# Margin check of a gated attention and expert kernel: its VectorE, ScalarE, TensorE and GpSimd pieces stand at other steps

## The chip, the cores and the metric

The kernel runs on one core of a Trainium2 chip. The metric is the device time of one execution in microseconds (us). Three runs of the kernel before gave 93.25, 93.72 and 95.69 us, median 93.72 us. One more execution, taken with the profiler, lasted 93.16 us; its span, from the first to the last instruction, is 91.4 us.

## The reference

Input x has 4 batches of 256 rows of 256 columns. It passes a gated layer pair and then a gated mixture of experts:

```
x = x + tanh(g_xattn) * GAT(ctx, adj = layernorm(x))      # two graph attention layers, 8 heads of 32
    e = leaky_relu(self + neigh) + -1e10 * (1 - adj);  alpha = softmax(e)
x = x + tanh(g_ffn) * MoE(layernorm(x))                   # 8 experts, hidden 128 each, top 2 of 8
    logits = tanh(xn @ Wg1.T) @ Wg2.T;  scores = softmax of the top 2, 0 elsewhere
    out = sum_e scores[e] * (silu(xn @ Wup[e].T + bup[e]) @ Wdown[e].T + bdown[e])
```

Since the mask factor is 1e10 and adj is a normalised row of x, the softmax picks in each row the column of the row's maximum, provided the maximum leads the second largest value by enough. The kernel uses that: it gathers rows by a one-hot matrix. The margin check proves that the lead of every row is large enough for the given weights. If it isn't, a general path recomputes everything.

## The kernel before

**Stages.** Up to about 30 us the kernel loads, finds each row's two largest values (`top`), builds the one-hot matrices and runs the two layers. Then `pe_experts`, `act_experts` and `dve_experts` run in step with each other, each as a loop over steps i written out by hand; the order of the calls in each is the order of that engine's queue. There are 32 work items (4 batches b of 8 experts e), and item k has its up product at step k (`pe_up`, L734 to L739), its SiLU on ScalarE at step k (L518), its weight broadcast (`pe_pick`, L756) at step k + 8, the product with it on VectorE (`dve_weigh`, writes `hid`, L1085) at step k + 8, the rounding copy on ScalarE (`act_hid`, L526) at step k + 8, the remainder (`dve_weigh_lo`, writes `hid_lo`, L1093) at step k + 9, and its down product (`pe_down`, L779 to L783) at step k + 11. Steps 32 and later have no up product.

**Once per batch.** The transposes of the next batch stand at e = 4 (`pe_xt`, L679), their rounding on ScalarE at e = 4 and the remainder `xt_lo` on VectorE (`dve_xt`, L1005) at e = 5. The router: gate product at e = 0 (`pe_gate`, L692), `dve_gate_sum` at e = 1, `dve_logits` at e = 2 (writes `lidx`), `scores` on GpSimd (L347 to L365), then two transposes on TensorE (`pe_score`, L700) and the copy `score_t` on VectorE (`dve_scores`, L1075) at e = 6. The first pick of the next batch, eight steps after the batch's first up product, waits for that copy. `dve_finish` (L1106) stands at e = 4 for the batch two behind.

**The margin check.** Its parts before the change:
- VectorE, step 13 (`check_peaks`, L1227 to L1233): maxima and sums of absolute values of ctx, W0, W1, the attention vectors and b0, six reductions, put into `peaks`. They stand ahead of `dve_xt` of step 13 and `score_t` of step 14.
- TensorE: transpose of `peaks` at the end of step 18 (`pe_peaks_turn`, L707), spread by a product with ones at the end of step 20 (`pe_peaks_spread`, L711). VectorE: `check_peak_max` at step 19 (L1238, L1241), `check_peaks_all` at step 21 (L1245).
- TensorE waits for `peaks_all` ahead of the score transposes of batch 2, step 22, since both use one PSUM bank.
- ScalarE: eight squares with row sums at steps 12 to 19 (L549).
- GpSimd: scores(2), `check_bound` (ten small operations), scores(3), `check_rows` (twelve small operations, each waiting for the one before). The first of `check_rows` waits for all eight squares.
- TensorE at step 37 (`pe_good_count`, L717) counts good rows, VectorE at step 38 makes the flag (L1250 to L1254), on which all engines branch.

Of the kernel before, what the change touches and what calls it, by code (L numbers as in the profile page):

```python
# [26 lines left out]
ALU = mybir.AluOpType  # L27
ACT = mybir.ActivationFunctionType
AX = mybir.AxisListType
# [7 lines left out]
B, N, D = 4, 256, 256  # L37
FIN = 64
H, FO = 8, 32
E, HE = 8, 128  # L40
T = B * N
NT = T // P
C = N // P
STEPS = B * E
# [3 lines left out]
SILU_SLOTS = PICK_LAG + 2  # L48
HID_SLOTS = 4
SCORE_PLACE = (3, 6, 6, 6)  # L50
WQ = 4
EQ = E // WQ
KS = 32 + 2 * E
# [9 lines left out]
def build(nc, x, ctx_t, w0, small, w1, bias_2, b0_r, b1_r, wup, wdown, bdown_2, check_w, avec, out):  # L63
    with ExitStack() as stack:
# [8 lines left out]
        ctx_sb = sb("ctx_sb", [P, T])  # L73
# [39 lines left out]
        peaks = sb("peaks", [P, P])  # L113
# [219 lines left out]
        def scores(pool, run, b):  # L333

            nb = run * B + b
            r = pair(b)
            done = [(run * (B - 1) + b - 1) * SCORE_STEPS]
            last = done[0] + SCORE_STEPS

            def link(ins, chained=True):  # L340
                done[0] += 1
                ins.then_inc(score_step, 1)
                if chained:
                    pool.wait_ge(score_step, done[0])

            pool.wait_ge(lidx_rdy, C * (nb + 1))
            link(nc.gpsimd.tensor_copy(lidx_f[:, r, 0:2], lidx[:, r, 0:2]))  # L347

            pool.wait_ge(lth_rdy, nb + 1)
            link(nc.gpsimd.tensor_scalar(prob[:, 0, r], lth[:, r], 0.5, 0.5, ALU.mult, ALU.add), False)  # L350
            link(nc.gpsimd.tensor_scalar(prob[:, 1, r], lth[:, r], -0.5, 0.5, ALU.mult, ALU.add))
            for k in range(2):
                for t in range(C * b, C * b + C):
                    link(nc.gpsimd.tensor_scalar(hit[:, k, t, :], expert_no[:], lidx_f[:, t, k:k + 1], prob[:, k, t:t + 1],
                                                 ALU.is_equal, ALU.mult), k == 1 and t == C * b + C - 1)
            link(nc.gpsimd.tensor_tensor(score[:, r, :], hit[:, 0, r, :], hit[:, 1, r, :], ALU.add))
            link(nc.gpsimd.tensor_copy(score_hi[:, r, :], score[:, r, :]))
            if run >= 1:
                pool.wait_ge(score_mm, run * B)
            if nb == 1:  # L360
                pool.wait_ge(score_zero, 1)
            hi, whole = (v.rearrange("p t (a e) -> p t a e", a=1).broadcast_to([P, C, 2, E])
                         for v in (score_hi[:, r, :].bitcast(F32), score[:, r, :]))
            nc.gpsimd.tensor_copy(score_parts[:, r, 0:2, 0:E], hi).then_inc(score_rdy, 1)
            nc.gpsimd.tensor_tensor(score_parts[:, r, 0:2, E:2 * E], whole, hi,  # L365
                                    ALU.subtract).then_inc(score_rdy, 1)
            assert done[0] == last

        @block.gpsimd
        def _(pool):  # L370
# [76 lines left out]
            def ts(o, a, *rest):  # L447
                link(nc.gpsimd.tensor_scalar(o, a, *rest))
# [17 lines left out]
            def check_rows():  # L466
                pool.wait_ge(xsq_rdy, NT)
                ts(rms[:], xsq[:], 1.0 / D, EPS, ALU.mult, ALU.add)
                tt(rms[:], rms[:], powers[:, NT:2 * NT], ALU.pow)
                tt(lead[:], top[:, :, 0], top[:, :, 1], ALU.subtract)  # L470
                ts(size[:], top[:, :, 0], -1.0, 0.0, ALU.mult, ALU.max)
                ts(good[:], top[:, :, 0], 0.0, None, ALU.max)
                tt(size[:], size[:], good[:], ALU.add)
                tt(size[:], size[:], rms[:], ALU.add)
                ts(size[:], size[:], 2e-6, None, ALU.mult)
                ts(need[:], rms[:], bound[:, 6:7], None, ALU.mult)
                tt(need[:], need[:], size[:], ALU.add)
                tt(lead[:], lead[:], need[:], ALU.subtract)
                nc.gpsimd.tensor_scalar(good[:], lead[:], 0.0, None, ALU.is_gt).then_inc(good_rdy, 1)

            scores(pool, 0, 2)
            check_bound()
            scores(pool, 0, 3)
            check_rows()

            def general():
                for b in range(B):
# [40 lines left out]
        def act_experts(act, run, extra):  # L528

            for i in range(STEPS + PICK_LAG):  # L530
                b, e = i // E, i % E
                if i < STEPS:
                    act_silu(act, run, i)
                    if b >= 1 and e == 2:
                        act_gate(act, run, b)
                    if b >= 1 and e == 3:
                        act_diff(act, run, b)
                if i >= PICK_LAG:
                    act_hid(act, run, i - PICK_LAG)
                if e == 2 and b + 1 < B:  # L540
                    act_norm(act, run, b + 1, range(C))
                if e == 4 and b + 1 < B:
                    act_xt(act, run, b + 1)
                for step in extra.get(i, ()):
                    step()
                if run == 0 and 12 <= i < 12 + NT:

                    t = i - 12
                    nc.scalar.activation(out_sq(t), x_sb[:, t, :], ACT.Square, accum_out=xsq[:, t:t + 1]).then_inc(xsq_rdy, 1)  # L549

        def out_sq(t):
# [151 lines left out]

        def pe_peaks_turn(pe):
            pe.wait_ge(peaks_rdy, 1)
            pe.wait_ge(gate_in_rdy, 3)
            nc.tensor.transpose(bank[:, ROUTE, CHECK_COL:CHECK_COL + P], peaks[:], ident[:]).then_inc(peaks_mm, 1)  # L707

        def pe_peaks_spread(pe):
# [79 lines left out]
        def pe_experts(pe, run, extra):  # L789

            for i in range(STEPS + DOWN_LAG):
                b, e = i // E, i % E
                if i < STEPS:
                    pe_up(pe, run, i)
                if PICK_LAG <= i < STEPS + PICK_LAG:
                    pe_pick(pe, run, i - PICK_LAG)
                for step in extra.get(i, ()):
                    step()
                if e == 0 and 1 <= b < B:
                    pe_gate(pe, run, b)  # L800
                if i >= DOWN_LAG:
                    pe_down(pe, run, i - DOWN_LAG)
                if e == 4 and b + 1 < B:
                    pe_xt(pe, run, b + 1)
                if b < B and e == SCORE_PLACE[b]:
                    if run == 0 and b == 2:
                        pe.wait_ge(peaks_all_rdy, 1)
                    pe_score(pe, run, b)
                if run == 0 and i == 2 * E + 2:
                    pe_peaks_turn(pe)  # L810
                if run == 0 and i == 2 * E + 4:
                    pe_peaks_spread(pe)
                if run == 0 and i == STEPS + 5:
                    pe_good_count(pe)
# [295 lines left out]
        def dve_experts(dve, run, extra):  # L1110

            for i in range(STEPS + PICK_LAG + 1):
# [13 lines left out]
                if b + 1 < B and e == (5 if b else 1):  # L1126
                    dve_xt(dve, run, b + 1)
                if b < B and e == SCORE_PLACE[b]:
                    dve_scores(dve, run, b)
# [3 lines left out]
        def _(dve):  # L1133
# [84 lines left out]
            gated(1)  # L1218
            dve_stats(dve, 0, 1)

            def check_peaks():

                w0t = check_sb[:, 0:C * FIN].rearrange("p (c k) -> p c k", c=C)
                w1t = check_sb[:, C * FIN:].rearrange("p (c k) -> p c k", c=C)
                dve.wait_ge(check_ld, 32)
                dve.wait_ge(peaks_part, 1)
                nc.vector.tensor_reduce(peaks[0:FIN, 0:1], ctx_sb[0:FIN, :], AX.X, ALU.max, apply_absolute_value=True).then_inc(peaks_part, 1)  # L1227
                nc.vector.tensor_reduce(colsum[:, 0:2], w0t, AX.X, ALU.add, apply_absolute_value=True).then_inc(peaks_part, 1)
                nc.vector.tensor_reduce(colsum[:, 2:4], w1t, AX.X, ALU.add, apply_absolute_value=True).then_inc(peaks_part, 1)
                nc.vector.tensor_reduce(peaks[0:H, 3:7], a_sb[:], AX.X, ALU.add, apply_absolute_value=True).then_inc(peaks_part, 1)  # L1230
                nc.vector.tensor_reduce(peaks[:, 7:8], b0_sb, AX.X, ALU.max, apply_absolute_value=True).then_inc(peaks_part, 1)
                dve.wait_ge(peaks_part, 6)
                nc.vector.tensor_reduce(peaks[:, 1:3], colsum[:].rearrange("p (k c) -> p k c", c=2), AX.X, ALU.max  # L1233
                                        ).then_inc(peaks_rdy, 1)
# [12 lines left out]
            def check_flag():  # L1247
# [6 lines left out]
                nc.vector.tensor_copy(flag[:], flag_f[:]).then_inc(flag_rdy, 1)  # L1254

            dve_experts(dve, 0, {0: [lambda: gated(2), lambda: dve_stats(dve, 0, 2)], 
                                 5: [lambda: gated(3), lambda: dve_stats(dve, 0, 3)], 13: [check_peaks],
                                 2 * E + 3: [check_peak_max], 2 * E + 5: [check_peaks_all], STEPS + 6: [check_flag]})

            def general():  # L1260

# [134 lines left out]
```

## Time and profile before

| | value |
|---|---|
| median of three runs (lowest, highest) | 93.72 us (93.25, 95.69) |
| the profiled execution: its time, its span | 93.16 us, 91.4 us |
| TensorE matmuls busy | 83.3 us (91%) |
| TensorE weight loads busy | 78.1 us (85%) |
| VectorE busy | 64.7 us (71%) |
| ScalarE busy | 55.2 us (60%) |
| GpSimd busy | 43.5 us (48%) |
| mean granted TensorE clock | 0.996 |

"Busy" is the time in which an engine works on any instruction. Matmuls overlap each other: a product of 256 columns is shown with 0.28 us, while in a dense stretch the next one starts about 0.12 us behind it. So whether TensorE is held up is read from the distance of two starts, not from the busy share. In a list in order of time, a bracket behind an instruction tells how long the engine was idle before it and what ended the idle time. Steps of the loops are found by counting the `hid` products of VectorE: that of item k is step k + 8.

### The profile page before, as it was taken

The numbers are of one execution on the slowest core, as the hardware profiler recorded it, in microseconds if no ns is written. First come the engines' busy times: TensorE is split into PE (matmuls) and PEld (weight loads), VectorE is DVE, ScalarE is ACT, GpSimd is POOL, SyncE is SP. The second block draws the span as 40 slices with busy tenths as digits, with TensorE's granted clock in tenths as the row PEclk, the third lists the DMA queues.
The fourth block names the chain that finished last, engine by engine and source line by source line (L and its number), as shares of the span: only waits on it lengthen the run. The fifth ranks groups of instructions, "written<-read, shape, count | busy, mean of one in ns | idle before, by whom it ended". The sixth has DMA issues, their size and how long they took to land.

```text
span 91.4 us, 1958 instructions
## 1 busy us (share of the span) xinstructions
PE 83.3 (91%) x615; PEld 78.1 (85%) x615; DVE 64.7 (71%) x202; ACT 55.2 (60%) x132; POOL 43.5 (48%) x95
## 2 busy tenths in 40 slices
PE   4959999989999999999999999999999999999800
PEld 4728888869899999989998999999999999999700
DVE  5887797857897609998599368795359767899520
ACT  1446888596695948398927799763366564433100
POOL 7970953698003999925900002885002988800000
PEclk9999999999999999999999999999999999999998
DMA  1999991000000000000000000030000030003021
GB/s 34 286 273 400 405 386 60 0 0 0 7 4 0 0 0 0 7 0 4 0 0 0 7 0 0 4 115 4 7 0 0 0 115 0 0 7 115 4 84 56
DMA packets 3339, 5.44 MB, mean 60 GB/s; under 512 B 474, under 2 KB 2748, under 8 KB 3068
## 3 DMA queue, kind: packets, MB, share of 16 engines
q1 hardware_dynamic: 3164, 5.00, 16.0%
q10 hardware_dynamic: 160, 0.26, 1.1%
q8 instruction: 7, 0.11, 0.5%
q14 instruction: 8, 0.07, 0.2%
HBM read 4.21 MB, written 1.05 MB: 58 GB/s over the span
## 4 chain that ended last, share of the span: by engine, by line
PE 59%; DVE 17%; DMA 6%; issue 6%; ACT 5%; DVEq 1%; POOL 1%; ACTq 1%
PE bank L734 6%; DMA ctx_sb<-in_ctx_t 6%; PE bank L735 6%; PE bank L739 6%; PE bank L896 6%; PE bank L781 5%; PE bank L872 5%; PE bank L783 5%; PE bank L782 5%; DVE hid_lo L1093 4%; PE bank L859 3%; PE bank L756 3%; DVE hid L1085 2%; PE bank L679 2%; DVE stat L990 2%
## 5 line engine op out<-in xcount | busy, mean ns | idle before, releaser
L1085 DVE TENSOR_TENSOR hid<-act_sb,bank 128x256 f32<-128x256 f32 x32 | 13.4, 418 | 10.9 <-PE bank L756 9.0
L518 ACT ACTIVATE act_sb<-bank,small_sb 128x256 f32<-128x256 f32 x32 | 15.1, 471 | 8.7 <-PE bank L739 8.4
L526 ACT CAST hid_hi<-hid 128x256 fp32r<-128x256 f32 x32 | 13.0, 405 | 10.7 <-DVE hid L1085 9.7
L781 PE MATMUL bank<-wdown_hi,hid_hi 128*128 128x256 f32 x64 | 18.4, 287 | 0.3 <-ACT hid_hi L526 0.3
L734 PE MATMUL bank<-xt_hi,wup_hi 128*128 128x256 f32 x64 | 18.0, 304 | 0.1
L783 PE MATMUL bank<-wdown_hi,hid_lo 128*128 128x256 f32 x64 | 18.1, 282 | 0.0
L782 PE MATMUL bank<-wdown_lo,hid_hi 128*128 128x256 f32 x64 | 18.0, 281 | 0.0
L735 PE MATMUL bank<-xt_hi,wup_lo 128*128 128x256 f32 x64 | 16.6, 281 | 0.0
L1093 DVE TENSOR_TENSOR hid_lo<-hid,hid_hi 128x256 fp32r<-128x256 f32 x32 | 13.4, 420 | 0.2
L739 PE MATMUL bank<-xt_lo,wup_hi 128*128 128x256 f32 x64 | 12.7, 280 | 0.0
L734 PEld LDWEIGHTS bank<-xt_hi,wup_hi 128*128 128x128 f32 x64 | 12.1, 189 | 0.5 <-ACT act_sb L518 0.3
L781 PEld LDWEIGHTS bank<-wdown_hi,hid_hi 128*128 128x128 f32 x64 | 12.0, 188 | 0.6 <-ACT hid_hi L526 0.5
L735 PEld LDWEIGHTS bank<-xt_hi,wup_lo 128*128 128x128 f32 x64 | 12.1, 189 | 0.1
L783 PEld LDWEIGHTS bank<-wdown_hi,hid_lo 128*128 128x128 f32 x64 | 12.1, 188 | 0.0
L782 PEld LDWEIGHTS bank<-wdown_lo,hid_hi 128*128 128x128 f32 x64 | 12.0, 188 | 0.0
L739 PEld LDWEIGHTS bank<-xt_lo,wup_hi 128*128 128x128 f32 x64 | 9.8, 188 | 0.0
L347 POOL CAST lidx_f<-lidx 128x4 f32<-128x4 uint32 x3 | 0.6, 188 | 19.1 <-DVE lidx L1035 19.1
L756 PE MATMUL bank<-score_t,pick 128*128 128x256 f32 x32 | 9.1, 285 | 0.1
L872 PE MATMUL bank<-w_sb,h 128*128 128x256 f32 x32 | 8.5, 389 | 0.0
L396 POOL TENSOR_SCALAR onehot<-x_sb,top 128x256 bf16<-128x256 f32 x6 | 5.5, 939 | 2.6 <-DVE top L1146 2.6
L756 PEld LDWEIGHTS bank<-score_t,pick 128*128 128x128 f32 x32 | 6.0, 188 | 0.4 <-DVE score_t L1075 0.4
L407 POOL TENSOR_TENSOR wup_lo<-wup_sb,wup_hi 128x512 fp32r<-128x512 f32 x4 | 5.1, 1280 | 2.6 <-ACT wup_hi L597 2.6
(147 smaller groups left out, 180.6 us busy)
## 6 DMA issues: line engine op xcount, KB each, us to landing
x_sb<-in_x SPq DMA_DIRECT2D x4, 256.0 KB, 5.1
wup_sb<-in_wup SPq DMA_DIRECT2D x1, 1024.0 KB, 7.2
wdown_sb<-in_wdown SPq DMA_DIRECT2D x1, 1024.0 KB, 9.4
out<-out_sb SPq DMA_DIRECT2D x3, 256.0 KB, 2.2
check_sb<-in_check_w SPq DMA_DIRECT2D x1, 320.0 KB
w_sb<-in_w SPq DMA_DIRECT2D x1, 256.0 KB, 5.5
out<-out_sb SPq DMA_DIRECT2D x2, 128.0 KB, 2.5
ctx_sb<-in_ctx_t ACTq DMA_DIRECT2D x1, 192.0 KB, 5.6
```

What stands on the lines that cost most here:

```text
L518: nc.scalar.activation(act_out(n), bank[:, UP[n % 2], 0:N], ACT.Silu, bias=bup_sb[:, k % E:k % E + 1]).then_inc(silu_rdy, 1)
L526: nc.scalar.copy(hid_hi[:, n % HID_SLOTS, :], hid[:, n % 2, :]).then_inc(hid_hi_rdy, 1)
L734: nc.tensor.matmul(dst, wup_hi[:, c, cols], xt_hi[:, b, c, :], start=(c == 0), stop=False)
L735: nc.tensor.matmul(dst, wup_lo[:, c, cols], xt_hi[:, b, c, :], start=False, stop=False)
L739: mm = nc.tensor.matmul(dst, wup_hi[:, c, cols], xt_lo[:, b, c, :], start=False, stop=(c == C - 1))
L756: nc.tensor.matmul(bank[:, PICK[n % 2], 0:N], pick[:, e, :], score_t[:, b, :], start=True, stop=True).then_inc(pick_mm, 1)
L781: nc.tensor.matmul(dst, hid_hi[:, n % HID_SLOTS, part], wdown_hi[:, e, :], start=False, stop=False, skip_group_check=True)
L782: nc.tensor.matmul(dst, hid_hi[:, n % HID_SLOTS, part], wdown_lo[:, e, :], start=False, stop=False, skip_group_check=True)
L783: mm = nc.tensor.matmul(dst, hid_lo[:, n % HID_SLOTS, part], wdown_hi[:, e, :], start=False, stop=(e == E - 1), skip_group_check=True)
L872: nc.tensor.matmul(dst, h1[:, b, c, t * P:(t + 1) * P], w1_sb[:, c, :], start=(c == 0), stop=False)
L1085: nc.vector.tensor_tensor(hid[:, n % 2, :], act_out(n), bank[:, PICK[n % 2], 0:N], ALU.mult).then_inc(hid_rdy, 1)
L1093: nc.vector.tensor_tensor(hid_lo[:, n % HID_SLOTS, :], hid[:, n % 2, :], hid_hi[:, n % HID_SLOTS, :].bitcast(F32), ALU.subtract).then_inc( ...
```

## The change

The pieces of the margin check get other places. VectorE: the six reductions become three calls, ctx at step 16, W0 and W1 at step 19, and the rest with the final reduction at step 22. Peak transposition and what follows move by one batch: TensorE from steps 18 and 20 to 26 and 28, VectorE from 19 and 21 to 27 and 29, and TensorE's wait for `peaks_all` from the score transposes of batch 2 to those of batch 3. The squares stand at ScalarE's steps 13 to 16 and 21 to 24. On GpSimd the order becomes scores(2), eight operations of `check_rows`, scores(3), `check_bound`, and the last four operations as `check_lead`. No operation is added or left out; no transfer changes.

```diff
--- before.py
+++ after.py
@@ -48,6 +48,7 @@
 SILU_SLOTS = PICK_LAG + 2
 HID_SLOTS = 4
 SCORE_PLACE = (3, 6, 6, 6)
+SQUARE_STEPS = (13, 14, 15, 16, 21, 22, 23, 24)
 WQ = 4
 EQ = E // WQ
 KS = 32 + 2 * E
@@ -473,15 +474,18 @@
                 tt(size[:], size[:], good[:], ALU.add)
                 tt(size[:], size[:], rms[:], ALU.add)
                 ts(size[:], size[:], 2e-6, None, ALU.mult)
+
+            def check_lead():
                 ts(need[:], rms[:], bound[:, 6:7], None, ALU.mult)
                 tt(need[:], need[:], size[:], ALU.add)
                 tt(lead[:], lead[:], need[:], ALU.subtract)
                 nc.gpsimd.tensor_scalar(good[:], lead[:], 0.0, None, ALU.is_gt).then_inc(good_rdy, 1)
 
             scores(pool, 0, 2)
+            check_rows()
+            scores(pool, 0, 3)
             check_bound()
-            scores(pool, 0, 3)
-            check_rows()
+            check_lead()
 
             def general():
                 for b in range(B):
@@ -543,9 +547,9 @@
                     act_xt(act, run, b + 1)
                 for step in extra.get(i, ()):
                     step()
-                if run == 0 and 12 <= i < 12 + NT:
-
-                    t = i - 12
+                if run == 0 and i in SQUARE_STEPS:
+
+                    t = SQUARE_STEPS.index(i)
                     nc.scalar.activation(out_sq(t), x_sb[:, t, :], ACT.Square, accum_out=xsq[:, t:t + 1]).then_inc(xsq_rdy, 1)
 
         def out_sq(t):
@@ -703,7 +707,7 @@
 
         def pe_peaks_turn(pe):
             pe.wait_ge(peaks_rdy, 1)
-            pe.wait_ge(gate_in_rdy, 3)
+            pe.wait_ge(gate_in_rdy, B)
             nc.tensor.transpose(bank[:, ROUTE, CHECK_COL:CHECK_COL + P], peaks[:], ident[:]).then_inc(peaks_mm, 1)
 
         def pe_peaks_spread(pe):
@@ -803,12 +807,12 @@
                 if e == 4 and b + 1 < B:
                     pe_xt(pe, run, b + 1)
                 if b < B and e == SCORE_PLACE[b]:
-                    if run == 0 and b == 2:
+                    if run == 0 and b == B - 1:
                         pe.wait_ge(peaks_all_rdy, 1)
                     pe_score(pe, run, b)
-                if run == 0 and i == 2 * E + 2:
+                if run == 0 and i == 3 * E + 2:
                     pe_peaks_turn(pe)
-                if run == 0 and i == 2 * E + 4:
+                if run == 0 and i == 3 * E + 4:
                     pe_peaks_spread(pe)
                 if run == 0 and i == STEPS + 5:
                     pe_good_count(pe)
@@ -1218,15 +1222,18 @@
             gated(1)
             dve_stats(dve, 0, 1)
 
-            def check_peaks():
-
+            def check_ctx():
+                dve.wait_ge(peaks_part, 1)
+                nc.vector.tensor_reduce(peaks[0:FIN, 0:1], ctx_sb[0:FIN, :], AX.X, ALU.max, apply_absolute_value=True).then_inc(peaks_part, 1)
+
+            def check_weights():
                 w0t = check_sb[:, 0:C * FIN].rearrange("p (c k) -> p c k", c=C)
                 w1t = check_sb[:, C * FIN:].rearrange("p (c k) -> p c k", c=C)
                 dve.wait_ge(check_ld, 32)
-                dve.wait_ge(peaks_part, 1)
-                nc.vector.tensor_reduce(peaks[0:FIN, 0:1], ctx_sb[0:FIN, :], AX.X, ALU.max, apply_absolute_value=True).then_inc(peaks_part, 1)
                 nc.vector.tensor_reduce(colsum[:, 0:2], w0t, AX.X, ALU.add, apply_absolute_value=True).then_inc(peaks_part, 1)
                 nc.vector.tensor_reduce(colsum[:, 2:4], w1t, AX.X, ALU.add, apply_absolute_value=True).then_inc(peaks_part, 1)
+
+            def check_small():
                 nc.vector.tensor_reduce(peaks[0:H, 3:7], a_sb[:], AX.X, ALU.add, apply_absolute_value=True).then_inc(peaks_part, 1)
                 nc.vector.tensor_reduce(peaks[:, 7:8], b0_sb, AX.X, ALU.max, apply_absolute_value=True).then_inc(peaks_part, 1)
                 dve.wait_ge(peaks_part, 6)
@@ -1254,8 +1261,8 @@
                 nc.vector.tensor_copy(flag[:], flag_f[:]).then_inc(flag_rdy, 1)
 
             dve_experts(dve, 0, {0: [lambda: gated(2), lambda: dve_stats(dve, 0, 2)], 
-                                 5: [lambda: gated(3), lambda: dve_stats(dve, 0, 3)], 13: [check_peaks],
-                                 2 * E + 3: [check_peak_max], 2 * E + 5: [check_peaks_all], STEPS + 6: [check_flag]})
+                                 5: [lambda: gated(3), lambda: dve_stats(dve, 0, 3)], 16: [check_ctx], 19: [check_weights], 22: [check_small],
+                                 3 * E + 3: [check_peak_max], 3 * E + 5: [check_peaks_all], STEPS + 6: [check_flag]})
 
             def general():
```

## Rows read from the trace of the kernel before

**Rows 1.** the chain of waits from 42 to 52 us: start us, us, what.
```profile
45.20 1.12 DVE peaks L1227
...
49.20 0.39 PE bank L756
```

**Rows 2.** TensorE in order of time (start, us, line, operation): steps 16 and 24.
```profile
48.66 0.40 PE L739 MATMUL bank<-xt_lo,wup_hi 128*128 128x256 f32 x2
...
49.43 0.17 PE L692 MATMUL bank<-wg_parts,xt_hi 128*128 128x16 f32 x1
...
63.51 0.40 PE L739 MATMUL bank<-xt_lo,wup_hi 128*128 128x256 f32 x2
...
63.87 0.18 PE L692 MATMUL bank<-wg_parts,xt_hi 128*128 128x16 f32 x1
```

**Rows 3.** one window of four microseconds: length, then busy us (instructions) by engine, clock.
```profile
72.00:76.00 4.00, 4.00 (x37) 4.00 (x36) 2.89 (x8) 2.03 (x5) 3.61 (x8) 1.00 0.19 66
```

**Rows 4.** VectorE in order of time: start, us, line, operation, idle before it.
```profile
45.12 1.21 DVE L1227 TENSOR_REDUCE peaks<-ctx_sb 64x1 f32<-64x1024 f32 x1
...
46.25 0.27 DVE L1228 TENSOR_REDUCE colsum<-check_sb 128x2 f32<-128x128 f32 x1
...
47.04 0.26 DVE L1230 TENSOR_REDUCE peaks<-a_sb 8x4 f32<-8x128 f32 x1
...
47.47 0.68 DVE L1005 TENSOR_TENSOR xt_lo<-bank,xt_hi 128x512 fp32r<-128x512 f32 x1
...
52.12 0.42 DVE L1085 TENSOR_TENSOR hid<-act_sb,bank 128x256 f32<-128x256 f32 x1 [1.42 <-PE bank L756]
...
56.27 0.28 DVE L1238 TENSOR_REDUCE peak_max<-bank 128x1 f32<-128x128 f32 x1
...
57.08 0.42 DVE L1085 TENSOR_TENSOR hid<-act_sb,bank 128x256 f32<-128x256 f32 x1 [0.20 <-PE bank L756]
...
62.58 0.42 DVE L1085 TENSOR_TENSOR hid<-act_sb,bank 128x256 f32<-128x256 f32 x1 [0.47 <-PE bank L756]
...
71.41 0.42 DVE L1085 TENSOR_TENSOR hid<-act_sb,bank 128x256 f32<-128x256 f32 x1 [0.63 <-PE bank L756]
```

**Rows 5.** ScalarE in order of time: a square, and the copy ahead of step 24's slot.
```profile
49.89 0.41 ACT L549 ACTIVATE h<-x_sb 128x256 f32<-128x256 f32 x1
...
64.58 0.41 ACT L526 CAST hid_hi<-hid 128x256 fp32r<-128x256 f32 x1 [0.16 <-DVE hid L1085]
```

**Rows 6.** GpSimd in order of time: check_bound's ends, scores(3), check_rows.
```profile
60.19 0.74 POOL L445 TENSOR_TENSOR bound<-peaks_all 128x1 f32<-128x1 f32 x3
...
62.99 0.40 POOL L448 TENSOR_SCALAR bound<-bound 128x1 f32<-128x1 f32 x1
...
70.26 0.19 POOL L347 CAST lidx_f<-lidx 128x4 f32<-128x4 uint32 x1 [6.87 <-DVE lidx L1035]
...
74.08 0.20 POOL L448 TENSOR_SCALAR rms<-xsq 128x8 f32<-128x8 f32 x1
74.37 1.67 POOL L445 TENSOR_TENSOR rms<-rms,powers 128x8 f32<-128x8 f32 x1
...
78.38 0.57 POOL L448 TENSOR_SCALAR need<-rms,bound 128x8 f32<-128x8 f32 x1
...
79.83 0.25 POOL L479 TENSOR_SCALAR good<-lead 128x8 f32<-128x8 f32 x1
```

**Rows 7.** TensorE in order of time: end of step 28, of step 30, row count.
```profile
71.74 0.29 PE L783 MATMUL bank<-wdown_hi,hid_lo 128*128 128x256 f32 x1
...
74.94 0.38 PE L700 MATMUL bank<-ident,score_parts 128*128 128x128 f32 x2
...
81.91 0.28 PE L717 MATMUL bank<-good,ones 128*128 128x8 f32 x2
```

**Rows 8.** the instructions that write hid_lo, over the whole span.
```profile
L1093 DVE TENSOR_TENSOR hid_lo<-hid,hid_hi x32: 416/419/444, 39.1 to 85.2; 128x256 fp32r<-128x256 f32 x32
```

**Rows 9.** the chain of waits from 76 us to the end.
```profile
76.03 0.13 PE bank L756
```

## The prediction

> **What bounds the kernel now.** I read the windows first, then the chain of waits, then single engines in order of time. In the expert stage TensorE is busy without a gap [rows 3] at the full granted clock (1.00, its 2.4 GHz level). Products of 256 columns start 0.12 us apart, and the next step's products stand ready in the queue. There, work on another engine costs time only if TensorE arrives at a wait too early.
>
> The chain of waits names the check nevertheless. From 45.20 us it runs through the reductions of step 13 and comes back to TensorE at the pick of 49.20 us [rows 1]. Read as a sum, it charges some 2.4 us to the check. I read it otherwise: a chain says who ended last, not how long the receiver had been waiting. TensorE's starts tell that [rows 2]. Step 16 has its last two up products from 48.66 us, and the gate product behind the pick starts at 49.43 us: 0.77 us. The same pair in step 24 is 63.51 and 63.87 us: 0.36 us. The difference, **0.41 us**, is all that TensorE lost to the blocked VectorE: it waited for the copy `score_t` of batch 1, which stood behind the reductions and `xt_lo` [rows 4]. Of the 2.35 us block, the rest was covered by the eight steps between up product and pick.
>
> From 76.03 us the chain leaves TensorE at the pick of item 24 [rows 9] and goes down VectorE to the end. That stretch keeps its instructions and starts when TensorE gets there, so it moves with TensorE.
>
> **The change part by part.** Clock readings are those of the trace before.
>
> *Step 13 of VectorE is cleared.* The block is 45.12 to 47.47 us [rows 4], 2.35 us. Without it, `xt_lo` starts at 45.12 and `score_t` needs only the transposes of step 14; the pick of step 16 finds it ready. Gain: 0.41 us.
>
> *Step 16 gets the ctx maximum*, 46.25 - 45.12 = 1.13 us by starts. The `hid` product of step 17 is preceded by 1.42 us of idle time [rows 4], which covers it by 0.29 us. If the cover were gone, `hid` would come later, but TensorE needs it two picks on, a whole step. Cost 0.
>
> *Step 19 gets the W0 and W1 sums*, 47.04 - 46.25 = 0.79 us, and loses the peak maximum and diagonal, 57.08 - 56.27 less 0.20 idle = 0.61 us [rows 4]. Net 0.18 against 0.20 of idle time. Cost 0.
>
> *Step 22 gets the small reductions*, 47.47 - 47.04 = 0.43 us, ahead of batch 2's `score_t`. Step 23's `hid` has 0.47 us of idle before it [rows 4]. `score_t` is wanted at the pick of step 24, a step later. Cost 0. Step 21 loses the small copy of the peaks.
>
> *The peak products at steps 26 and 28.* On VectorE, the 0.61 us at step 27 lies in the 0.63 us of idle before step 28's `hid` at 71.41 [rows 4], so the diagonal is ready at 71.41 - 0.63 + 0.61 = 71.39 us. TensorE has issued step 28 at 71.74 + 0.12 = 71.86 us [rows 7] and then waits for the diagonal: 0.47 us to spare. TensorE's own instructions are as many as before; they only change step. This cover is the thinnest on TensorE's queue: behind that wait stand all products of step 29. If it failed entirely, the loss would be of the size of the small VectorE piece, at most 0.61 us. Taken: 0. The wait for `peaks_all` now stands ahead of the transposes of step 30; the copy is made in step 29, a step earlier, so 0.
>
> *Squares.* A square takes 0.41 us [rows 5], and ScalarE has idle time in steps 21 to 24: the rounding copy of step 24 starts at 64.58, ends at 64.99, and the step's square ends by about 65.5 us with its row sum (0.41 and an estimate of 0.1 for the read-out). Only the GpSimd work waits for it. Cost 0.
>
> *GpSimd's new order.* `scores(3)` now stands behind eight operations that wait for the last square. They take 78.38 - 74.08 = 4.30 us [rows 6]. From 65.5 they end at 69.8 us; `scores(3)` starts at 70.26 when `lidx` is there. Slack 0.46 us. `scores(3)` runs until `check_rows` starts at 74.08, and TensorE asks for it at 74.94 [rows 7]: 0.86 us more. So 1.32 us of slack in all. Cost 0; the other end is the second rival. `check_bound` (62.99 + 0.40 - 60.19 = 3.20 us) and the last four operations (79.83 + 0.25 - 78.38 = 1.70 us) follow from 74.08 and end at 78.98 us, before 80.08 as now, and before TensorE's count at 81.91 us [rows 6, 7]. The tail doesn't notice.
>
> *A rule against GpSimd's step.* The longest operation of `check_rows` is one of 1.67 us at 74.37 [rows 6]. VectorE made `hid_lo` beside it, and all 32 of those took 0.416 to 0.444 us [rows 8]: VectorE doesn't pay. On GpSimd, operations of one shape (128x8) range up to 0.57 us, the one at 78.38 [rows 6]. The Trainium skill, page "SBUF — State Buffer", section "Who interferes with whom", says that a VectorE instruction with two SBUF inputs and a GpSimd instruction that reads SBUF exclude one another for the whole instruction, whichever began first. On VectorE's side the trace disagrees with it (0.444 us at most). On GpSimd's side the rule would make the sum that of the second rival below.
>
> *Sum.* -0.41 us, bounds -0.61 (the last 0.2 for small gaps that I can't see, since some matmul records may be missing: my estimate) and +0.20 (the thin cover at step 28 gone: +0.61). The profiled execution had 93.16 us (span 91.4, 1.76 around it); it becomes 92.75. The median of the runs shown lies 0.56 above the profiled time, by which it would be 93.31. I take the middle, **93.0 us**, as the forecast.
>
> **The rivals.** *First: the whole block was on the path.* The chain of waits [rows 1] speaks for it; then 2.35 us go and the time is 93.16 - 2.35 = 90.8 us. Against it stands that TensorE issued at its usual distance until 48.66 us. Chance 0.03.
>
> *Second: GpSimd's new order makes scores(3) late.* Its place is TensorE's wait ahead of the two transposes of step 30; behind it stand the up products of step 31. If each of the eight operations waits for one VectorE instruction of 0.42 us, `check_rows` takes 4.30 + 8 x 0.42 = 7.66 us, 3.36 too long; less the slack of 1.32, TensorE stands 2.0 us, and the sum is 93.16 - 0.41 + 2.0 = 94.8 us. It decides from 1.32 us of delay, and makes the kernel over 2% slower from 1.32 + 0.41 + 1.87 = 3.6 us. Against it: the 4.30 us were measured beside VectorE's densest stretch, with two instructions of 0.42 us in every step, and contain such waits already. Chance 0.08, a third of it over 2%.
>
> *Third: the gain is eaten by a small new stall*, at step 28's diagonal or by late `hid` products, 0.2 to 0.6 us. The time is 93.0 to 93.4 us in the profile's frame, and no difference is seen. Chance 0.20. That the change doesn't do what it says is not in question: all of it is a new order of the same calls.
>
> **How the numbers follow.** My forecast has 0.69, the rivals 0.03, 0.08 and 0.20. The range takes the forecast and the third rival, from 92.75 - 0.2 - 0.1 = 92.4 in the profile's frame (0.1 for executions: the profiled one and the lowest run, 93.25, differ by that) to 93.4 + 0.56 = 94.0 in the median's frame, and a little of the second: 92.4 to 94.2. A measurement of this kernel can tell about 2%, 1.9 us, from no change. Faster by that needs the first rival: 0.03. Slower needs the second at its far end, or a median caught by runs such as the 95.69 us: 0.05. Within: 0.92.
>
> **What the profile of the changed kernel would show.** Right: the gate product of step 16 stands 0.36 us behind the last up products; `score_t` of batch 1 comes right behind its transposes; no idle of TensorE after the diagonal at step 28 or before the transposes of step 30; the tail from the pick of item 24 as long as now; the span near 91.0 us. Wrong: a start distance above 0.3 us ahead of the spread product or the transposes of step 30, `lidx_f` of batch 3 later than `lidx`, or a tail of another length.

## The result and the profile after

The changed kernel's median is 93.17 us (92.45 to 95.06, 20 runs), the kernel before's 93.41 us (92.87 to 95.69, 20 runs). The ratio, which leaves out the runs disturbed on either side, is 0.9951, 95% interval [0.9928, 0.9974]: 0.46 us less (0.24 to 0.67). Forecast were 0.41 us less and 93.0 us.

The whole span compares badly here. The changed kernel's first profile (94.00 us, span 92.2) is longer than the one before, and a second one (92.77 us, span 90.9) is shorter. So I measure the **stretch** from the first copy `score_t` (step 3, when the loads are done) to the first of the last two output operations (`out_sb`), which stands beside TensorE's last products. On VectorE in order of time (start, us, line, operation) its ends are, before:

```profile
34.87 0.41 DVE L1075 CAST score_t<-bank 128x256 fp32r<-128x256 f32 x1
...
86.52 0.88 DVE L1106 SCALAR_TENSOR_TENSOR out_sb<-bank,gates,xa 128x256 f32<-128x256 f32 x2 [0.93 <-PE bank L783]
```

and in the changed kernel's first profile, from which all rows of this section are:

```profile
34.89 0.41 DVE L1079 CAST score_t<-bank 128x256 fp32r<-128x256 f32 x1
...
86.12 0.88 DVE L1110 SCALAR_TENSOR_TENSOR out_sb<-bank,gates,xa 128x256 f32<-128x256 f32 x2 [0.93 <-PE bank L787]
```

51.65 us before, 51.23 after: **0.42 us less**. The second profile has 51.26. That the first one's span is longer comes from behind the last product, from the issue of the two output stores on the DMA queue of SyncE; before, first and second profile after:

```profile
87.03 1.46 SPq L306 DMA_DIRECT2D out<-out_sb  x2
```

```profile
86.64 2.95 SPq L307 DMA_DIRECT2D out<-out_sb  x2
```

```profile
86.56 1.55 SPq L307 DMA_DIRECT2D out<-out_sb  x2
```

1.46, 2.95 and 1.55 us for the same two stores; neither kernel has changed them.

TensorE in order of time, around step 16 and step 24, answers to [rows 2]:

```profile
48.69 0.40 PE L743 MATMUL bank<-xt_lo,wup_hi 128*128 128x256 f32 x2
48.92 0.28 PE L760 MATMUL bank<-score_t,pick 128*128 128x256 f32 x1
49.04 0.18 PE L696 MATMUL bank<-wg_parts,xt_hi 128*128 128x16 f32 x1
...
62.79 0.40 PE L743 MATMUL bank<-xt_lo,wup_hi 128*128 128x256 f32 x2
...
63.15 0.17 PE L696 MATMUL bank<-wg_parts,xt_hi 128*128 128x16 f32 x1
```

Step 16 now needs 49.04 - 48.69 = 0.35 us where it needed 0.77, as much as step 24 (0.36). VectorE, the pieces of the check and what follows each, answers to [rows 4]:

```profile
46.87 0.42 DVE L1079 CAST score_t<-bank 128x256 fp32r<-128x256 f32 x1
...
49.97 1.21 DVE L1227 TENSOR_REDUCE peaks<-ctx_sb 64x1 f32<-64x1024 f32 x1
51.73 0.42 DVE L1089 TENSOR_TENSOR hid<-act_sb,bank 128x256 f32<-128x256 f32 x1 [0.56 <-PE bank L760]
...
56.07 0.68 DVE L1234 TENSOR_REDUCE colsum<-check_sb 128x2 f32<-128x512 f32 x1
56.66 0.41 DVE L1089 TENSOR_TENSOR hid<-act_sb,bank 128x256 f32<-128x256 f32 x1
...
62.22 0.42 DVE L1089 TENSOR_TENSOR hid<-act_sb,bank 128x256 f32<-128x256 f32 x1 [0.60 <-ACT act_sb L522]
...
70.31 0.29 DVE L1248 TENSOR_SCALAR peak_diag<-ident,peak_max 128x128 f32<-128x128 f32 x1
70.79 0.42 DVE L1089 TENSOR_TENSOR hid<-act_sb,bank 128x256 f32<-128x256 f32 x1 [0.20 <-PE bank L760]
```

In the kernel before, `score_t` of batch 1 and the pick that waited for it stood here:

```profile
48.73 0.42 DVE L1075 CAST score_t<-bank 128x256 fp32r<-128x256 f32 x1
...
49.20 0.39 PE L756 MATMUL bank<-score_t,pick 128*128 128x256 f32 x1
```

`score_t` of batch 1 starts at 46.87 instead of 48.73 us. Behind the ctx maximum 0.56 us of idle time are left, behind the diagonal 0.20 us. Behind the W sums none is left: the `hid` product of step 20 starts 0.45 us behind its pick at 56.21 us, where 0.37 us is usual, so it is 0.08 us late. GpSimd in order of time, first and last of `check_rows`' first part, of `scores(3)`, and of the rest, answers to [rows 6]:

```profile
64.77 0.20 POOL L449 TENSOR_SCALAR rms<-xsq 128x8 f32<-128x8 f32 x1 [5.17 <-ACT h L553]
...
68.57 0.24 POOL L449 TENSOR_SCALAR size<-size 128x8 f32<-128x8 f32 x1
69.55 0.19 POOL L348 CAST lidx_f<-lidx 128x4 f32<-128x4 uint32 x1 [0.75 <-DVE lidx L1039]
...
72.99 0.43 POOL L366 TENSOR_TENSOR score_parts<-score,score_hi 128x32 f32<-128x32 f32 x1
73.46 0.73 POOL L446 TENSOR_TENSOR bound<-peaks_all 128x1 f32<-128x1 f32 x3
...
77.66 0.24 POOL L482 TENSOR_SCALAR good<-lead 128x8 f32<-128x8 f32 x1
```

And TensorE where the two waits stand that were in doubt, ends of steps 28 and 30, answers to [rows 7]:

```profile
71.13 0.28 PE L787 MATMUL bank<-wdown_hi,hid_lo 128*128 128x256 f32 x1
71.25 0.28 PE L715 MATMUL bank<-peak_diag,ones 128*128 128x8 f32 x2
...
74.43 0.28 PE L787 MATMUL bank<-wdown_hi,hid_lo 128*128 128x256 f32 x1
74.55 0.38 PE L704 MATMUL bank<-ident,score_parts 128*128 128x128 f32 x2
```

Both follow 0.12 us behind the product before them: no wait. The chain's last pick, item 24, answers to [rows 9]:

```profile
75.64 0.14 PE bank L760
```

From it to the last outputs it is 86.12 - 75.64 = 10.48 us; before, 86.52 - 76.03 = 10.49. The tail moved and did not shrink.

### The profile page after: what moved, and what is told of

Its sections match the earlier page's. It is cut to its first block, busy times and chain, and to the rows that moved or that the text cites. A ratio compares the mean times of both kernels' runs of the same rounds, so it can differ in the third digit from the quotient of the medians.

```text
span 92.2 us, 1957 instructions
## 1 busy us (share of the span) xinstructions
PE 83.3 (90%) x615; PEld 78.0 (85%) x615; DVE 64.5 (70%) x202; ACT 55.9 (61%) x132; POOL 42.9 (47%) x95
## 4 chain that ended last, share of the span: by engine, by line
PE 61%; DVE 16%; issue 5%; ACT 5%; DMA 5%; DVEq 1%; POOL 1%
PE bank L738 7%; PE bank L739 7%; PE bank L743 7%; PE bank L785 6%; PE bank L787 6%; PE bank L900 6%; PE bank L786 5%; PE bank L876 5%; DMA bias_sb<-in_bias 5%; DVE hid_lo L1097 4%; PE bank L760 3%; PE bank L683 2%; DVE hid L1089 2%; DVE stat L994 2%; PE bank L697 1%
## 5 line engine op out<-in xcount | busy, mean ns | idle before, releaser
L876 PEld LDWEIGHTS bank<-w_sb,h 128*128 128x128 f32 x32 | 5.5, 190 | 1.3 <-issue 0.9
L330 POOL TENSOR_TENSOR rstd<-veps,powers 128x2 f32<-128x2 f32 x4 | 2.8, 711 | 7.2 <-DVE nmean L1000 7.1
```

The costliest lines, as they stand in the source:

```text
L876: nc.tensor.matmul(dst, h1[:, b, c, t * P:(t + 1) * P], w1_sb[:, c, :], start=(c == 0), stop=False)
```

## The experiments

All are measured by the stretch in their profile (one execution each, which agrees within 0.03 us between the two profiles of the changed kernel), and by the time ratio to the kernel before with its 95% interval.

| kernel | stretch, us | against before | time ratio |
|---|---|---|---|
| before | 51.65 | | |
| changed (first, second profile) | 51.23, 51.26 | -0.42, -0.39 | 0.9951 [0.9928, 0.9974], again 0.9977 [0.9941, 1.0013] |
| reductions left out | 51.22 | -0.43 | 0.9966 [0.9916, 1.0017] |
| reductions twice | 53.92 | +2.27 | 1.0343 [1.0242, 1.0444] |
| one piece at step 15 | 51.26 | -0.39 | 1.0016 [0.9962, 1.0070] |
| squares and rows only | 51.63 | -0.02 | 0.9963 [0.9925, 1.0002] |
| reductions only | 58.43 | +6.78 | 1.0794 [1.0716, 1.0872] |
| changed, one power operation more | 51.24 | -0.41 | 1.0060 [1.0022, 1.0098] |
| changed, two more | 52.89 | +1.24 | 1.0217 [1.0141, 1.0294] |
| changed, late flag | 50.90 | -0.75 | 0.9896 [0.9844, 0.9947] |
| one piece at 15, late flag | 50.90 | -0.75 | 0.9932 [0.9882, 0.9982] |
| changed, late flag, four buffers | 50.53 | -1.12 | 0.9956 [0.9897, 1.0016] |
| one piece at 15, late flag, four buffers | 50.49 | -1.16 | 0.9919 [0.9871, 0.9967] |

The timed ratios don't tell the small differences apart. The kernels whose stretch is 0.39 to 0.43 us shorter (changed, reductions left out, one piece at 15, one power operation more) have ratios from 0.9951 to 1.0060, and the one with squares and rows only, whose stretch is not shorter, has 0.9963. What a part brings is read from the stretch alone.

**Reductions left out.** To the kernel before:

```diff
 def check_peaks():
-    nc.vector.tensor_reduce(peaks[0:FIN, 0:1], ...)  # and four more
+    nc.vector.tensor_reduce(peaks[:, 7:8], b0_sb, ...).then_inc(peaks_rdy, 1)
```

> The kernel before with five of the six reductions of step 13 left out (only the maximum of b0 is made, so the margin check tests a smaller bound than it should). Slack theory: VectorE work ahead of score_t costs only what exceeds its slack, which was 0.41 us of the 2.35 us; so about 0.4 us less than the kernel before, the same as the kernel with the change, and the gate product of step 16 stands 0.36 us behind the last up products. Rival, the whole block is on the path: 2.2 us less (2.35 less 0.13 for the reduction that stays).

TensorE around step 16:

```profile
48.45 0.40 PE L739 MATMUL bank<-xt_lo,wup_hi 128*128 128x256 f32 x2
...
48.80 0.18 PE L692 MATMUL bank<-wg_parts,xt_hi 128*128 128x16 f32 x1
```

The gap is gone (0.35 us), and the stretch is 0.43 us shorter. Leaving 2.22 us of work out brings what moving it brings (0.43 and 0.42 us, the same within 0.03). The rival (2.2 us) falls, with it the chain of waits as a price list.

**Reductions twice.** The first five are made a second time.

```diff
     dve.wait_ge(peaks_part, 6)
+    (the same five reductions once more)
+    dve.wait_ge(peaks_part, 11)
```

> The kernel before with the first five reductions of step 13 made a second time, 2.28 us more by the distance of their starts. Slack theory: the slack is used up, so all of it is paid, 2.3 us more than the kernel before, and TensorE loses 0.41 + 2.28 = 2.7 us at the pick of step 16. Together with the run without reductions this shows a threshold: 2.2 us less work gives 0.4, 2.3 us more work costs 2.3. Rival, the loss at step 16 is a fixed cost of that step and has nothing to do with the block: no difference.

TensorE in the same place:

```profile
48.19 0.28 PE L735 MATMUL bank<-xt_hi,wup_lo 128*128 128x256 f32 x1
50.12 0.50 PE L739 MATMUL bank<-xt_lo,wup_hi 128*128 128x256 f32 x2 [1.65 <-DVE xt_lo L1005]
51.12 0.39 PE L756 MATMUL bank<-score_t,pick 128*128 128x256 f32 x1 [0.49 <-DVE score_t L1075]
51.34 0.17 PE L692 MATMUL bank<-wg_parts,xt_hi 128*128 128x16 f32 x1
```

2.27 us more for 2.28 us of work: behind the threshold all is paid. In step 16 TensorE needed 51.34 - 48.19 = 3.15 us where 0.36 + 0.12 are undisturbed: it lost 2.67 us (expected 2.7). The size came out, the place only in part: most of the wait is now one position earlier, at `xt_lo`, which I had not named. Both copies stand behind the block.

**One piece at step 15.**

```diff
-13: [check_peaks],
+15: [check_peaks],
```

> The kernel before with the six reductions moved in one piece from step 13 to step 15, behind score_t of batch 1; nothing else differs. Slack theory: the block of 2.35 us then stands before no copy that TensorE waits for soon, and hid of step 16 comes some 1.5 us later, while TensorE needs it two picks on; so 0.4 us less than the kernel before, as much as the whole change gives, and no splitting is needed. Rival, the split matters: the late hid of step 16 holds up the pick of step 18 or ScalarE's copy, and the time is that of the kernel before or up to 0.5 us more.

VectorE, first reduction and the `hid` product behind the block:

```profile
48.14 1.20 DVE L1227 TENSOR_REDUCE peaks<-ctx_sb 64x1 f32<-64x1024 f32 x1
...
50.59 0.42 DVE L1085 TENSOR_TENSOR hid<-act_sb,bank 128x256 f32<-128x256 f32 x1
```

`hid` of step 16 stands 50.59 - 48.14 = 2.45 us behind the start of the block. ScalarE's rounding copy stands idle for 1.74 us until it comes, but no product of TensorE waits: the stretch is 0.39 us shorter, as with the whole change. One edited number does it; the splitting is not needed for the gain. The timed ratio does not show the gain; its interval ends just short of -0.4%.

**Squares and rows only.** The kernel before with the change's `SQUARE_STEPS` on ScalarE and `check_lead` behind `check_bound` on GpSimd.

> The kernel before with only the ScalarE and GpSimd parts of the change: the squares at steps 13 to 16 and 21 to 24, check_rows in two parts with its first eight operations ahead of scores(3). The reductions stay at step 13 in one piece. Slack theory: no difference to the kernel before (within 0.1 us), since neither part touches score_t of batch 1. Rival, part of the gain comes from ScalarE steps 17 to 19 that are freed of squares or from GpSimd's shorter tail: 0.2 to 0.4 us less.

TensorE around step 16:

```profile
48.30 0.40 PE L742 MATMUL bank<-xt_lo,wup_hi 128*128 128x256 f32 x2
...
49.04 0.17 PE L695 MATMUL bank<-wg_parts,xt_hi 128*128 128x16 f32 x1
```

The gap is there as before (0.74 us), the stretch the same (-0.02). These parts bring nothing of their own.

**Reductions only.** The other half: the changed kernel with ScalarE and GpSimd as before.

```diff
 scores(pool, 0, 2)
-check_rows()
-scores(pool, 0, 3)
 check_bound()
-check_lead()
+scores(pool, 0, 3)
+check_rows()
```

> The changed kernel with ScalarE's squares and GpSimd's order as before (scores(2), check_bound, scores(3), check_rows); the VectorE and TensorE parts of the change stay. check_bound then waits for the peaks of step 29, ready at 73.4 us in the changed kernel's profile, and stands ahead of scores(3): 73.4 + 3.2 + 3.9 = 80.5 us, where TensorE wants the scores at 74.55 us. Queue theory: TensorE stands 5.9 us ahead of the transposes of step 30, and the time is 5.5 us above the kernel before, near 98.9 us. Rival, GpSimd's order is off the path: 0.4 us less than the kernel before.

It costs 6.78 us instead of 5.5. TensorE ahead of the transposes of step 30, at them, two starts of the next step and a later pick:

```profile
74.08 0.28 PE L785 MATMUL bank<-wdown_hi,hid_lo 128*128 128x256 f32 x1
79.49 0.66 PE L702 MATMUL bank<-ident,score_parts 128*128 128x128 f32 x2 [5.13 <-POOL score_parts L366]
...
80.38 0.41 PE L736 MATMUL bank<-xt_hi,wup_hi 128*128 128x256 f32 x1
80.59 0.41 PE L737 MATMUL bank<-xt_hi,wup_lo 128*128 128x256 f32 x1
...
84.07 0.28 PE L758 MATMUL bank<-score_t,pick 128*128 128x256 f32 x1
```

and the windows (length, busy us by engine, granted clock, DMA):

```profile
74.00:79.60 5.60, 0.47 (x5) 0.29 (x4) 0.50 (x2) 0.45 (x2) 4.54 (x19) 0.77 0.00 0
79.60:82.00 2.40, 2.40 (x12) 2.40 (x13) 0.69 (x2) 0.47 (x1) 2.14 (x4) 0.50 0.00 0
...
86.00:90.00 4.00, 4.00 (x37) 4.00 (x36) 3.56 (x11) 1.46 (x5) 0.00 (x0) 1.00 0.09 31
```

The queue theory holds: the wait is 5.13 us long and GpSimd ends it. What I had missed is what comes with it. While TensorE stands idle, the granted clock falls to 0.50 (the 1.2 GHz level; 0.50 from 77.5 us on), starts behind the wait are 0.21 us apart in place of 0.12, and from 84 us it is 1.00 again. The same pick in the changed kernel:

```profile
77.14 0.28 PE L760 MATMUL bank<-score_t,pick 128*128 128x256 f32 x1
```

The wait makes 79.49 - 74.08 - 0.12 = 5.29 us (5.9 were expected). From the transposes to this pick it is 84.07 - 79.49 = 4.58 us, in the changed kernel 77.14 - 74.55 = 2.59: 1.99 us for the clock. With the 0.42 us won at step 16 the sum is 5.29 + 1.99 - 0.42 = 6.86, against 6.78 measured. So GpSimd's new order is no ornament: once the peaks come at steps 26 to 29, it is what keeps the change from costing 8% (ratio 1.0794).

**One and two power operations more**, a probe of GpSimd's slack in the changed kernel:

```diff
 tt(rms[:], rms[:], powers[:, NT:2 * NT], ALU.pow)
+tt(need[:], rms[:], powers[:, NT:2 * NT], ALU.pow)   # once, or twice
```

> The changed kernel with one more power operation of 1.75 us (start to start) among the eight operations ahead of scores(3); its result is overwritten later. In the changed kernel's profile check_rows' first part ends at 68.81 us, lidx lets scores(3) start at 69.55, and its end at 73.42 is 1.13 us ahead of the transposes at 74.55 us: 0.74 + 1.13 = 1.87 us of slack. Queue theory: 1.75 us just fit, no difference to the changed kernel (0 to 0.2 us). Rival, the slack is the 1.32 us of the prediction: 0.4 us more than the changed kernel. Rival, any delay of scores(3) is paid: 1.0 us more.

> The changed kernel with two more power operations, 3.50 us, ahead of scores(3). Queue theory with 1.87 us of slack: 1.6 us more than the changed kernel, all of it as a gap of TensorE ahead of the transposes of step 30. Rival, GpSimd's place is off the path: no difference.

One leaves the stretch at 51.24 us, two make it 52.89, 1.66 more than the changed kernel. With two, TensorE at the end of step 30:

```profile
74.30 0.28 PE L789 MATMUL bank<-wdown_hi,hid_lo 128*128 128x256 f32 x1
76.04 0.41 PE L706 MATMUL bank<-ident,score_parts 128*128 128x128 f32 x2 [1.46 <-POOL score_parts L366]
```

76.04 - 74.30 less the usual 0.12 is 1.62 us, by the rule 3.50 - 1.87 = 1.63. The agreement to 0.01 us is luck. In this trace the first part of `check_rows` grew by 3.42 us (72.09 - 64.63 = 7.46 against 4.04) and `scores(3)` took 3.74 us in place of 3.87, so TensorE's 1.62 us leave a slack of 3.42 - 0.13 - 1.62 = 1.67 us: the 1.87 less the hand-overs, 0.06 us to `scores(3)` and 0.15 us to TensorE. With one operation more the scores were ready at 75.54 us, 0.40 ahead of the transposes at 75.94.

The timed ratio of the first (1.0060) is 1.1% above that of the changed kernel, which is what the rival "any delay is paid" (1.0 us) forecast. Its trace speaks against that rival: the transposes start 75.94 - 75.83 = 0.11 us behind the product before them. In this profile the first `score_t` starts at 36.29 us where the other kernels have 34.42 to 35.87, and the stores' issue took 3.08 us: its excess lies outside the stretch. The timed runs have no trace, and where their excess lies is open.

**Late flag.** The tail runs down VectorE, and the flag is the last work there that doesn't belong to the outputs. It moves two steps back:

```diff
-STEPS + 6: [check_flag]
+STEPS + PICK_LAG: [check_flag]
```

> The changed kernel with check_flag on VectorE moved from step 38 to step 40, behind the last hid_lo, where VectorE is idle for 0.93 us before the last output. The three small operations (83.32 to 83.88 us by starts, 0.56 us) stand in the stretch from the pick of item 24 to the end that runs down VectorE. Chain theory: hid of item 31 comes 0.56 us earlier and the end with it, until TensorE's own products bind; TensorE's gaps there are 0.1 and 0.44 us, so 0.4 to 0.55 us less than the changed kernel and 0.8 to 1.0 less than the kernel before. Rival, TensorE is the bound in the tail too: no difference to the changed kernel.

The stretch falls by 0.33 us to 50.90, less than the 0.4 to 0.55 forecast. TensorE's wait of 0.44 us ahead of its last products shrinks to 0.10, and another of 0.10 stays (starts at 83.97 and 84.19, at 84.85 and 85.07, 0.22 us apart in place of 0.12). VectorE at the end:

```profile
85.41 0.16 DVE L1257 TENSOR_REDUCE flag_f<-bank 128x1 f32<-128x8 f32 x1
...
86.41 0.88 DVE L1110 SCALAR_TENSOR_TENSOR out_sb<-bank,gates,xa 128x256 f32<-128x256 f32 x2 [0.47 <-PE bank L787]
```

The flag now lies in idle time, of which 0.47 us are left ahead of the last outputs. This kernel is also faster by time: 0.9896 [0.9844, 0.9947].

**One piece at 15 with the late flag**: those two edited numbers in the kernel before, nothing of the change otherwise.

> The kernel before with two edits of one number each: the six reductions in one piece at step 15 and check_flag at step 40; peaks, squares and GpSimd's order stay as before. Slack theory: the stretch from the first hid to the last out_sb is shorter than before by 0.39 (one piece at 15) and 0.33 us (late flag), 48.29 - 0.72 = 47.6 us, the same as for the changed kernel with the late flag (47.54). Rival, the split and the new order give something of their own when the tail is shorter: 0.1 us or more behind that kernel.

50.90 us, the same as the changed kernel with the late flag. (The expectation counts from the first `hid`; from there it is 85.32 - 37.78 = 47.54 us, expected 47.6.)

**Four buffers for hid**, on top of the changed kernel with the late flag:

```diff
-hid = sb("hid", [P, 2, N])
+hid = sb("hid", [P, 4, N])
-if n >= 2: wait hid_hi_rdy, hid_lo_rdy for n - 1
+if n >= 4: wait hid_hi_rdy, hid_lo_rdy for n - 3
```

> The changed kernel with check_flag at step 40 and four buffers for hid in place of two, so that a hid product no longer waits for the hid_lo right ahead of it on VectorE. Chain theory: in the tail the distance of two hid products falls from 0.89 us to TensorE's 0.83 us, and the two gaps of 0.1 us that TensorE still has there close; the stretch from the first hid to the last out_sb is 0.2 us shorter than with the late flag alone, 47.35 us. Rival, the gaps of 0.1 us come from the copy on ScalarE and not from VectorE's wait: no difference to 47.54 us.

VectorE in the tail:

```profile
77.70 0.42 DVE L1089 TENSOR_TENSOR hid<-act_sb,bank 128x256 f32<-128x256 f32 x1
...
78.53 0.42 DVE L1089 TENSOR_TENSOR hid<-act_sb,bank 128x256 f32<-128x256 f32 x1
```

The products are 0.83 us apart (0.89 before), so the mechanism is right. The gain is 0.37 us in place of 0.2: each of TensorE's gaps had also made the start behind it late (84.19 to 84.38 us with the late flag, 0.19 in place of 0.12), which the estimate left out. The timed ratio, 0.9956 [0.9897, 1.0016], doesn't show this gain.

**The changed kernel again**, and last the **three small edits together** on the kernel before:

> The changed kernel once more, on the chip of the other two. All theories: stretch from the first hid to the last out_sb 47.87 us as in its first profile (48.29 before), gate product of step 16 0.36 us behind the last up products; time 0.4 to 0.5 us below the kernel before.

> The kernel before with three edits: the six reductions in one piece at step 15, check_flag at step 40, four buffers for hid. Counted from the first score_t to the last out_sb, the profiles gave 51.65 us for the kernel before, 51.23 for the changed kernel, 50.90 with the late flag and 50.53 with the late flag and four buffers. Slack theory: 50.5 us here too, 1.1 us less than before (-0.4 at step 16, -0.33 late flag, -0.37 buffers), time ratio near 0.988, with none of the change's other moves. Rival, the hid products that come late behind the block at step 15 (1.3 us later than in the changed kernel) meet the four buffers otherwise: 50.7 us or more.

The second profile of the changed kernel has 51.26 us, and its time ratio (0.9977) has an interval that takes in both -0.4% and no difference. The three edits give 50.49 us as expected and a ratio of 0.9919 [0.9871, 0.9967]. By the stretch it is the shortest kernel of all, 1.16 us under the one before and 0.74 under the changed one; by time its interval overlaps with that of the late flag alone, and I don't rank the two.

## Why the prediction was right

*The price of the block, -0.41 us.* Right in size (0.42 by the stretch) and cause. The run without reductions, the one with the block alone elsewhere, and the one with the other half of the change alone pin it to the two copies behind the block. That the timed ratio gives nearly the same (0.46 us) is in part luck: the same kernel measured again gave 0.9977, 0.21 us, with no difference inside its interval. The reading that gave it was the distance of TensorE's starts, not the chain, whose 2.4 us were the first rival.

*The covers at steps 16, 19 and 22.* The cost of 0 was right, the covers themselves only at step 16. 0.56 us of idle time stayed behind the ctx maximum (forecast 0.29), since VectorE no longer comes late out of step 14. Behind the W sums the cover failed by 0.08 us (forecast 0.02 to spare). At step 23 it failed too: `hid` started at 62.22 us, 0.74 us behind its pick at 61.48, where the kernel before had 0.37 (62.58 and 62.21). The profile names a ScalarE operation, but the moved squares are not the cause: with the reductions only, and the squares at their old steps, it is 0.74 us as well, and with squares and rows only it is 0.37. With four buffers for `hid` it is 0.38. So it hangs on the small reductions at step 22 together with the two buffers; by which path is open. Nothing was paid for either, because TensorE needs `hid` later, which is the reason that the prediction gave for step 16.

*Step 28.* The diagonal was ready at 70.31 + 0.29 = 70.60 us, TensorE wanted it at 71.25: 0.65 us of slack, forecast 0.47.

*GpSimd.* The first part took 68.81 - 64.77 = 4.04 us (forecast 4.30). The slack was 69.55 - 68.81 = 0.74 us to `lidx` and 74.55 - 73.42 = 1.13 us to the transposes, 1.87 in all against 1.32; the power probes give 1.67 usable. Of the 0.55 us more, 0.26 are the shorter first part. Most of the rest is that TensorE, which now has the peak products in steps 26 and 28, came to the transposes 74.55 - 63.15 = 11.40 us behind the gate product of step 24, before 74.94 - 63.87 = 11.07. The second rival's price was right in kind: 3.50 us of delay cost 1.66. Its rule from the Trainium skill (page "SBUF — State Buffer", "Who interferes with whom") stayed without effect on the time. The longest `hid_lo` of the changed kernel took 0.464 us, the eight operations together less than before.

*The tail moves as it is.* Right: 10.48 against 10.49 us.

*The forecast time.* The step that was left loose is the frame: the profiled execution against the median. 93.0 was the middle of the two, and that 93.17 came out so near is luck: the median of the kernel before was 93.41 us over 20 runs, 0.31 below that of the three runs on which the frame rested. The sign "span near 91.0 us" failed in the first profile (92.2) and held in the second (90.9), with the same stretch in both: that difference is head and stores.

## What to carry to other kernels

Price a block on a side engine by the distance of starts on the engine that bounds, beside an undisturbed step; the chain of waits names the block but charges it with time that slack had paid. When a check's parts are moved later, look at every queue in which something urgent stands behind them: here the old order on GpSimd would have cost 8%. Before splitting a block, look for one place behind the urgent copies that takes it whole.

## What the runs showed of the hardware

- In the wait of 5.13 us TensorE's granted clock fell from 1.00 to 0.50. It was still 0.50 from 79.6 to 82 us, though the engine was busy again, with products 0.21 us apart, and 1.00 from 84 us on. It cost 1.99 us beside the wait itself. In the wait of 1.46 us, in the run with two power operations, it stayed at 1.00, and from 76.41 us on starts were 0.12 us apart.
- A short wait costs more than its length: the product behind one (0.39 us long in the row, 0.28 otherwise) delays the next start by some 0.1 us. Of the 0.41 us at step 16, 0.30 were wait and 0.11 this (pick to gate product 49.43 - 49.20 = 0.23 us in place of 0.12).
- The issue of the same two output stores took from 1.02 us (three small edits) to 3.09 us (two power operations more). This spread of 2.07 us is more than the stretches of the kernels without an added wait differ (1.16 us).
